# A two-layer perceiver kernel: the latents as chunk 0 of the second cross attention's loop, high and low parts of the first one rearranged, and a weight split placed later

## The chip, the cores and the metric

The kernel runs on one core of a Trainium2 chip. The metric is the device time of one execution in microseconds. Median before: 2354.21 us of 3 runs (2351.45 to 2356.31). The engines are called as the profile calls them, with their roles: PE is TensorE (matmuls), PEld its weight loads, DVE is VectorE, ACT is ScalarE, POOL is GpSimd, SP is SyncE, which only issues DMAs here.

## The reference

Four batches of 128 latents of width 512 (`x`) attend to a context of 4 x 2048 rows (`ctx_1024`). Six sublayers follow each other, each added to `x`; the three that the change touches are shown.

```python
# 1: cross attention with "stablemax", 16 heads of 32
def stablemax(x):
    s = jnp.where(x >= 0, x + 1.0, 1.0 / (1.0 - x))
    return s / jnp.sum(s, axis=-1, keepdims=True)
x = x + L0_xattn(layernorm(x), ctx)          # softmax replaced by stablemax
x = x + L0_attn(layernorm(x))                # causal linear attention
# 3: feed-forward with fake quantisation by the maximum of the whole tensor
def act_fake_quant(x, clip_factor):
    scale = jax.nn.sigmoid(clip_factor) * jnp.max(jnp.abs(x)) / 127.0
    return jnp.clip(round(x / scale), -128.0, 127.0) * scale
h = act_fake_quant(silu(gate(xq)) * up(xq), clip_down)
# 4: perceiver attention, 16 heads of 64
xn, ln = layernorm(x_ctx, g, b), layernorm(latents, g, b)
q = ln @ Wq
kv = jnp.concatenate((xn, ln), axis=1) @ Wkv  # context and latents are keys
sim = where(mask_full, q @ k.T * scale, -max) # the latents' part is unmasked
out = layernorm(softmax(sim) @ v @ Wout, g, b)
x = x + L1_attn(layernorm(x)); x = x + L1_ffn(layernorm(x))
```

## The kernel before, in words

Every sublayer is one or more `Block`s: each engine has its own instruction list in a block, and all engines meet at its end. Inside a block, engines wait for each other by semaphores only, and each engine keeps the order in which its list is written. Matmuls with fp32 accuracy are done as three fp16 ones: a value is scaled and rounded to a high part (`_hi`), what is left is the low part (`_lo`), and hi x hi, hi x lo and lo x hi are added in PSUM.

**First cross attention** (`context_attention_0`). 8192 context rows are taken in 16 chunks of 512. A chunk has 8 units (`UNITS`), each half of the heads for 128 keys, 1024 columns wide. Per unit u of chunk c: PE makes scores (L611) into one of two pairs of banks; ACT and DVE form stablemax as max(s+1, exp(-ln(1+relu(-s)))): Relu (L475), Ln (L478), Exp (L481) on ACT and the maximum with the scores on DVE (`larger`, L530). In units 2 and 6 (`MIN_ON_DVE`) DVE takes the minimum instead of ACT's Relu (L524), and ACT goes on with Ln (L471). POOL rounds the result to `p_hi` (L419); the low part `p_lo` is made by DVE (L537), in units 3 and 7 (`LOW_ON_POOL`) by POOL (L424). Three units later (`LAG`) PE multiplies by the values (L626). In the same stream PE projects keys and values of chunk c+1, one of 8 products per unit (L593, L597); ACT and DVE split each product (L452, L459; L507, L513). Context rows of chunk c+2 are split too, high part on POOL (L412, behind `p_hi` of units 1 to 4), low part on DVE (L500, in slots 4 to 7). DVE's list in slot u of a chunk is: minimum of u (if 2 or 6), `larger` of u-1, split of product u-1, low part of u-2, sums of the chunk before (slot 2), context low part (slots 4 to 7).

**Feed-forward of layer 0** (`quantised_ffn_0`, L972 to L1106). POOL's list: memset, first `partition_all_reduce` (the maximum over partitions), then for both next weights (`wk`, `wv` of the second cross attention) scale, round to high, subtract to low (L980, L983, L986), then the second `partition_all_reduce`. DVE waits for the second one, then quantises h in 22 scalar operations (L1058, L1061); ACT and PE follow.

**Second cross attention** (`context_attention_1`). After queries are made, a block of its own handles the latents as keys: 16 projections (8 of keys, 8 of values), then per batch plain scores for a running maximum (L1389), the maximum (L1463), a spread of it by DMA into a diagonal (L1326, L1318), scores less the maximum (L1292, L1300), exponential (L1441), `p_hi` on POOL (L1365), `p_lo` on DVE (L1493), outputs (L1310), copy to `acc` (L1485). A second block runs over 16 context chunks c. Ahead of its loop stand normalisation of chunks 0 and 1 (moments and a Newton step on DVE, L1674 to L1698, the scaling on POOL, L1553), their turn by PE (L1872), and the projections of chunk 0 with its plain scores (L1882). In iteration c, 16 units of chunk c (scores, Exp L1649, POOL L1584, DVE L1764, outputs) stand beside the 16 projections of chunk c+1 (`mm_keys` L1244, `mm_values` L1254, split by L1611, L1618, L1710, L1717), its plain scores, and the turn of chunk c+2. Products, plain scores and turns share a ring of 4 PSUM banks in a fixed order (`RING_ORDER`).

Of the kernel before, what the change touches and what calls it, by code (L numbers as in the profile page):

```python
# [5 lines left out]
P = 128  # L6
# [219 lines left out]
def context_attention_0(nc, g, d):  # L226
# [6 lines left out]
    MIN_ON_DVE = (2, 6)  # L233
    LOW_ON_POOL = (3, 7)
    with ExitStack() as ctx:
# [101 lines left out]
        with ExitStack() as sub:  # L337
# [15 lines left out]
            min_done, p_done, p_hi_done = s.sem("min_done"), s.sem("p_done"), s.sem("p_hi_done")  # L353
            low_v, low_p = s.sem("low_v"), s.sem("low_p")
            outputs, acc_done = s.sem("outputs"), s.sem("acc_done")

            ON_ACT = [u for u in range(UNITS) if u not in MIN_ON_DVE]
            LOW_ON_DVE = [u for u in range(UNITS) if u not in LOW_ON_POOL]

            def place(c, u, units):  # L360

                return len(units) * c + len([x for x in units if x <= u])

            def low_wait(eng, c, u):

                if u in LOW_ON_POOL:
                    eng.wait_ge(low_p, place(c, u, LOW_ON_POOL))
                else:
                    eng.wait_ge(low_v, place(c, u, LOW_ON_DVE))

# [9 lines left out]
            with nc.Block() as block:  # L380
# [25 lines left out]
                def _(pool):  # L406
# [15 lines left out]
                    def p_low(c, u):  # L422
                        pool.wait_ge(p_hi_done, UNITS * c + u + 1)
                        nc.gpsimd.tensor_tensor(p_lo[:, u % 4, :], r[:, u % 4, :], p_hi[:, u % 4, :], ALU.subtract)\  # L424
                            .then_inc(low_p, 1)

# [11 lines left out]
                    for c in range(NCH):  # L438
                        for u in range(UNITS):
                            p_high(c, u)  # L440
                            if u in LOW_ON_POOL:
                                p_low(c, u)
                            if c + 2 < NCH and 1 <= u < KT + 1:
                                context_hi(c + 2, u - 1)

                @block.scalar
                def _(act):
# [17 lines left out]
                    def below_zero(c, u):  # L465

                        if before(c, u, 4):
                            low_wait(act, *before(c, u, 4))
                        if u in MIN_ON_DVE:
                            act.wait_ge(min_done, place(c, u, MIN_ON_DVE))  # L470
                            nc.scalar.activation(r[:, u % 4, :], r[:, u % 4, :], ACT.Ln, scale=-1.0, bias=1.0)\  # L471
                                .then_inc(ln_done, 1)
                        else:
                            act.wait_ge(scores, UNITS * c + u + 1)
                            nc.scalar.activation(r[:, u % 4, :], bank_pair(u), ACT.Relu, scale=-1.0, bias=1.0)\  # L475
                                .then_inc(neg_done, 1)
                            act.wait_ge(neg_done, place(c, u, ON_ACT))
                            nc.scalar.activation(r[:, u % 4, :], r[:, u % 4, :], ACT.Ln, bias=1.0)\  # L478
                                .then_inc(ln_done, 1)
# [16 lines left out]
                def _(dve):  # L496
# [21 lines left out]
                    def below_zero(c, u):  # L518

                        if u in MIN_ON_DVE:  # L520
                            dve.wait_ge(scores, UNITS * c + u + 1)
                            if before(c, u, 4):
                                low_wait(dve, *before(c, u, 4))
                            nc.vector.tensor_scalar(r[:, u % 4, :], bank_pair(u), -1.0, 0.0, ALU.add, ALU.min)\  # L524
                                .then_inc(min_done, 1)

# [6 lines left out]
                    def p_low(c, u):  # L533
                        if u in LOW_ON_POOL:
# [3 lines left out]
                            .then_inc(low_v, 1)  # L538
# [14 lines left out]
                    for c in range(NCH):  # L553
                        for u in range(UNITS):
                            below_zero(c, u)
# [1930 lines left out]
```

## Time and profile before

| what | us |
|---|---|
| median of the runs shown | 2354.21 |
| the profiled execution, and its span | 2355.0, 2353.2 |
| loop of the first cross attention, from its first score | 90.85 to 633.4 |
| feed-forward block of layer 0 | 824.4 to 896.3 |
| block of the latents as keys | 950.3 to 1053.2 |
| context block up to its loop | 1053.5 to 1118.4 |
| its loop, 16 iterations | 1118.4 to 2037.3 |

Busy over the whole span: PE 85%, DVE 69%, ACT 41%, POOL 32%. How to read the rows: times are microseconds from the span's start. In a timeline a row is start, length, engine, line of the kernel, operation, output<-inputs, shapes, how many were merged, and in brackets how long the engine sat idle before and what released it. A row of busy time by stretch has the stretch and its length, then busy time and instructions of PE, PEld, DVE, ACT and POOL, the granted PE clock as a share of full speed (1.00 is 2.4 GHz, 0.50 is 1.2 GHz), the DMA engines' share and GB/s. L12 is line 12 of the kernel before.

### The profile page before, as it was taken

How to read it: one execution, taken by the hardware profiler on the slowest of the kernel's cores; microseconds unless marked ns; L12 is line 12 of the kernel's file. 1: busy time of each engine (PE TensorE's matmuls, PEld its weight loads, DVE VectorE, ACT ScalarE, POOL GpSimd, SP SyncE). 2: the span in 40 equal slices, each digit the busy share in tenths (PEclk: the TensorE clock that was granted, in tenths of full speed). 3: DMA queues.
4: the chain of work that ended last, by engine and by line, in shares of the span. 5: the costliest groups of instructions: out<-in, count | busy, mean ns of one | idle time of the engine just before them, and what ended most of it. 6: DMA issues, size and time to landing. Idle time of an engine off the chain costs nothing. (4 is left out here: it accounts for less than half of the span.)

```text
span 2353.2 us, 44141 instructions
## 1 busy us (share of the span) xinstructions
PE 1994.2 (85%) x17800; PEld 1095.5 (47%) x17800; DVE 1629.5 (69%) x2826; ACT 962.8 (41%) x1373; POOL 743.5 (32%) x736
## 2 busy tenths in 40 slices
PE   3788988898589346848999999999999999667896
PEld 1355555555445223334555555555555555434542
DVE  3489888988754764255777777777777776535676
ACT  2477787877610322212333333333333333201332
POOL 2355555564410350012333333333333332212010
PEclk8899999999689567968999999999999999988898
DMA  4223323331220401000000000000000000110300
GB/s 136 64 72 91 91 57 80 91 76 43 55 108 24 170 1 36 20 2 22 26 16 20 20 21 21 21 21 21 21 21 21 20 21 1 46 68 0 148 1 18
DMA packets 39194, 106.16 MB, mean 45 GB/s; under 512 B 18384, under 2 KB 20688, under 8 KB 32848
## 3 DMA queue, kind: packets, MB, share of 16 engines
q1 hardware_dynamic: 38992, 103.35, 14.2%
q8 instruction: 141, 2.31, 0.4%
q14 instruction: 61, 0.50, 0.1%
HBM read 75.42 MB, written 1.05 MB: 32 GB/s over the span
## 5 line engine op out<-in xcount | busy, mean ns | idle before, releaser
L1584 POOL TENSOR_SCALAR a1c_p_hi<-a1c_pf 128x512 f16<-128x512 f32 x256 | 191.1, 747 | 622.5 <-ACT a1c_pf L1649 621.1
L419 POOL TENSOR_SCALAR a0c_p_hi<-a0c_r 128x1024 f16<-128x1024 f32 x128 | 153.1, 1196 | 254.7 <-DVE a0c_r L530 188.1
L1611 ACT ACTIVATE a1c_k_hi<-PS 128x512 f16<-128x512 f32 x128 | 76.5, 598 | 305.7 <-PE PS L1244 305.7
L1649 ACT ACTIVATE a1c_pf<-PS,a_maskc 128x512 f32<-128x512 f32 x256 | 175.2, 686 | 48.8 <-PE PS L1300 38.5
L1764 DVE TENSOR_TENSOR a1c_p_lo<-a1c_pf,a1c_p_hi 128x512 f16<-128x512 f32 x256 | 185.8, 727 | 5.2 <-POOL a1c_p_hi L1584 5.2
L1732 DVE CUSTOM_DVE_ANT_0 a1c_junk<-PS,a1c_maskr 128x512 bf16<-128x512 f32 x256 | 175.9, 687 | 19.2 <-DVE a1c_ctop L1732 1.0
L1618 ACT ACTIVATE a1c_v_hi<-PS 128x512 f16<-128x512 f32 x128 | 76.9, 601 | 244.5 <-PE PS L1254 195.2
L1710 DVE SCALAR_TENSOR_TENSOR a1c_k_lo<-PS,a1c_k_hi 128x512 f16<-128x512 f32 x128 | 88.3, 690 | 99.9 <-ACT a1c_k_hi L1611 99.9
L530 DVE TENSOR_TENSOR a0c_r<-PS,a0c_r 128x1024 f32<-128x1024 f32 x128 | 155.1, 1211 | 2.0 <-ACT a0c_r L481 2.0
L537 DVE TENSOR_TENSOR a0c_p_lo<-a0c_r,a0c_p_hi 128x1024 f16<-128x1024 f32 x96 | 151.5, 1578 | 0.0
L1244 PE MATMUL PS<-a_x_hi,w_wk_hi 128*128 128x512 f16 x544 | 141.2, 382 | 9.2 <-PEq L1203 4.5
L1717 DVE SCALAR_TENSOR_TENSOR a1c_v_lo<-PS,a1c_v_hi 128x512 f16<-128x512 f32 x128 | 88.5, 692 | 86.2 <-ACT a1c_v_hi L1618 84.8
L1310 PE MATMUL PS<-a1c_v_hi,a1c_p_hi 128*128 128x65 f16 x1088 | 129.7, 196 | 19.8 <-DVE a_acc L1485 13.4
L1244 PE MATMUL PS<-a_x_lo,w_wk_hi 128*128 128x512 f16 x544 | 141.4, 383 | 0.0
L1244 PE MATMUL PS<-a_x_hi,w_wk_lo 128*128 128x512 f16 x544 | 140.5, 381 | 0.0
L1254 PE MATMUL PS<-w_wv_lo,a_x_hi 128*128 128x512 f16 x544 | 139.6, 379 | 0.0
L1254 PE MATMUL PS<-w_wv_hi,a_x_lo 128*128 128x512 f16 x544 | 139.6, 379 | 0.0
L1254 PE MATMUL PS<-w_wv_hi,a_x_hi 128*128 128x512 f16 x544 | 139.3, 378 | 0.0
L481 ACT ACTIVATE a0c_r<-a0c_r 128x1024 f32<-128x1024 f32 x128 | 135.5, 1058 | 4.1
L1310 PEld LDWEIGHTS PS<-a1c_v_hi,a1c_p_hi 128*128 128x128 f16 x1088 | 101.0, 98 | 64.6 <-issue 27.6
L1310 PE MATMUL PS<-a1c_v_hi,a1c_p_lo 128*128 128x65 f16 x1088 | 128.8, 196 | 0.0
L1310 PE MATMUL PS<-a1c_v_lo,a1c_p_hi 128*128 128x65 f16 x1088 | 127.7, 195 | 0.0
(367 smaller groups left out, 4969.1 us busy)
## 6 DMA issues: line engine op xcount, KB each, us to landing
a_cf<-in_ctxT SPq DMA_DIRECT2D x16, 1024.0 KB, 5.2
a0c_ks<-a0c_k_hi SPq DMA_DIRECT2D x128, 128.0 KB, 2.3
a1c_cf<-in_ctx SPq DMA_DIRECT2D x16, 1024.0 KB, 4.9
a0c_ks<-a0c_k_lo SPq DMA_DIRECT2D x64, 128.0 KB, 2.4
f_w<-in_w SPq DMA_DIRECT2D x4, 1024.0 KB, 8.8
f_w<-in_w SPq DMA_DIRECT2D x1, 4096.0 KB, 19.9
s1q_w<-in_L1a_wT SPq DMA_DIRECT2D x3, 1024.0 KB, 7.5
w_gate_raw<-in_w_gate SPq DMA_DIRECT2D x1, 2816.0 KB, 9.5
```

The source lines that it names most:

```text
L419: nc.gpsimd.tensor_scalar(p_hi[:, u % 4, :], r[:, u % 4, :], 1.0, 0.0, ALU.mult, ALU.add)\
L481: nc.scalar.activation(r[:, u % 4, :], r[:, u % 4, :], ACT.Exp, scale=-1.0)\
L530: nc.vector.tensor_tensor(r[:, u % 4, :], bank_pair(u), r[:, u % 4, :], ALU.max)\
L537: nc.vector.tensor_tensor(p_lo[:, u % 4, :], r[:, u % 4, :], p_hi[:, u % 4, :], ALU.subtract)\
L1244: mm = nc.tensor.matmul(out, wk[i][:, k, f * P:(f + 1) * P], (x_hi, x_lo)[j][e][:, k, :], start=(step == 0), stop=(step == 11))
L1254: mm = nc.tensor.matmul(out, (x_hi, x_lo)[j][e][:, k, t * P:(t + 1) * P], wv[i][:, k, group * BANK:(group + 1) * BANK], start=(step == 0), ...
L1310: mm = nc.tensor.matmul(out(h, i), p[:, n % 4, i * P:(i + 1) * P], v[e][:, t, h, :], start=(first(h) and step == 0), stop=(last(h) and ste ...
L1584: nc.gpsimd.tensor_scalar(p_hi[:, v % 4, :], pf[:, v % 2, :], 1.0, 0.0, ALU.mult, ALU.add)\
L1649: nc.scalar.activation(pf[:, v % 2, :], g.PS[:, S0 + v % 2, :], ACT.Exp, bias=maskc[:, at:at + 1]).then_inc(exp_done, 1)
L1717: nc.vector.scalar_tensor_tensor(out=v_lo[e][at], in0=g.PS[:, ring_bank("values", c, n), :].rearrange("p (h n) -> p h n", h=8), scalar=UNS ...
L1732: nc.vector.tensor_tensor_reduce(junk[:], g.PS[:, ring_bank("plain", c, h), :], maskr[c % 2][:], 1.0, LOWEST, ALU.add, ALU.max, ctop[:, h: ...
L1764: nc.vector.tensor_tensor(p_lo[:, v % 4, :], pf[:, v % 2, :], p_hi[:, v % 4, :], ALU.subtract)\
```

## The change

Three edits. In the first cross attention every unit now has the Relu on ACT and the low part on DVE; `MIN_ON_DVE`, `LOW_ON_POOL` and their semaphores go.

```diff
-    MIN_ON_DVE = (2, 6)
-    LOW_ON_POOL = (3, 7)
...
                         for u in range(UNITS):
                             p_high(c, u)
-                            if u in LOW_ON_POOL:
-                                p_low(c, u)
                             if c + 2 < NCH and 1 <= u < KT + 1:
                                 context_hi(c + 2, u - 1)
...
-                        if u in MIN_ON_DVE:
-                            act.wait_ge(min_done, place(c, u, MIN_ON_DVE))
-                            nc.scalar.activation(r[:, u % 4, :], r[:, u % 4, :], ACT.Ln, scale=-1.0, bias=1.0)\
-                                .then_inc(ln_done, 1)
-                        else:
...
+                        act.wait_ge(scores, UNITS * c + u + 1)
+                        nc.scalar.activation(r[:, u % 4, :], bank_pair(u), ACT.Relu, scale=-1.0, bias=1.0)\
+                            .then_inc(neg_done, 1)
+                        act.wait_ge(neg_done, UNITS * c + u + 1)
+                        nc.scalar.activation(r[:, u % 4, :], r[:, u % 4, :], ACT.Ln, bias=1.0).then_inc(ln_done, 1)
...
                     def p_low(c, u):
-                        if u in LOW_ON_POOL:
-                            return
                         dve.wait_ge(p_hi_done, UNITS * c + u + 1)
```

In the feed-forward the split of the second weight stands behind the second reduction instead of before it.

```diff
                 for i in range(2):
                     pool.wait_ge(top_done, i + 1)
                     nc.gpsimd.partition_all_reduce(tops[:, i:i + 1], top[:, i:i + 1], P, reduced_max)\
                         .then_inc(all_done, 1)
-                    if i == 0:
-                        for n, (hi, lo) in enumerate(g.next_weights):
...
+                    next_weights(i)
```

In the second cross attention the latents' block goes. The loop runs over j = 0 to 16 (`NJ`): j = 0 is the latents, j >= 1 is context chunk j-1. The latents are projected ahead of the loop, with the turn of context chunk 0 in slots 11 to 14, and the normalisation of one context chunk instead of two. In iteration 0, each unit's outputs are a sum of their own that DVE copies to `acc` (`first_sums`, 16 copies of 260 columns, where 12 of up to 455 stood); its tops have their own tiles, one diagonal per batch, 8 spread DMAs of 4 times the size, and no mask. PE waits for the memsets of the ones before its first projection.

```diff
+    NJ = NCH + 1
...
+                    pe.wait_ge(ones_set, 4)
                     for v in range(UNITS):
                         if v % 2 == 0 and v >= 2:
                             plain_scores(0, v // 2 - 1)
                         project(0, v)
...
+                    for j in range(NJ):
                         for v in range(UNITS):
                             if v % 2 == 0:
-                                score(c, v)
+                                score(j, v)
...
-                            if c + 1 < NCH:
-                                project(c + 1, v)
+                            if j + 1 < NJ:
+                                project(j + 1, v)
...
+                    def first_sums(v):
+
+                        t, gp, side = tile_of(v), group_of(v), side_of(v)
+                        dve.wait_ge(outputs, v + 1)
+                        nc.vector.tensor_copy(acc[:, batch_at(0, t), 8 * gp + side:8 * gp + 8:2, :],
+                                              g.PS[:, O0 + side, 0:4 * W].rearrange("p (h n) -> p h n", h=4))\
+                            .then_inc(acc_done, 1)
...
+                        if j == 0:
+                            for b in range(B):
+                                build_diag(diag0[b], topx0[:, :, b, :], fs).then_inc(diag_done, 1)
+                            return
...
+                            if j == 0 and v >= 4:
+                                first_sums(v - 4)
+                            if j == 1 and v < 4:
+                                first_sums(UNITS - 4 + v)
...
+                        if j == 0:
+                            first, last = True, True
+                            if v >= 2:
+                                pe.wait_ge(acc_done, v - 1)
```

## Rows read from the trace of the kernel before

**Rows 1.** Busy time by stretch: first loop, latents' attention, second loop

```profile
296.00:331.00 35.00, 31.27 (x379) 18.82 (x377) 32.05 (x32) 27.70 (x32) 19.18 (x14) 1.00 0.28 77
...
995.00:1053.00 58.00, 26.18 (x464) 20.85 (x464) 32.29 (x56) 9.12 (x16) 9.71 (x16) 0.65 0.02 2
...
1236.00:1296.00 60.00, 60.00 (x629) 32.52 (x628) 44.88 (x102) 22.79 (x39) 19.33 (x26) 1.00 0.08 25
```

**Rows 2.** Timeline of PE, first cross attention, one chunk

```profile
299.98 1.04 PE L593 MATMUL PS<-a0c_c_hi,a_wk_hi 128*128 128x512 f16 x4 [2.10 <-DVE a0c_c_lo L500]
...
323.12 0.62 PE L611 MATMUL PS<-a_qs,a0c_ks 98*128 98x128 f16 x8 [1.56 <-DVE a0c_r L530]
...
333.78 1.04 PE L593 MATMUL PS<-a0c_c_hi,a_wk_hi 128*128 128x512 f16 x4 [2.10 <-DVE a0c_c_lo L500]
```

**Rows 3.** Timeline of DVE, first cross attention, the same chunk

```profile
301.58 1.21 DVE L537 TENSOR_TENSOR a0c_p_lo<-a0c_r,a0c_p_hi 128x1024 f16<-128x1024 f32 x1
...
307.48 1.22 DVE L524 TENSOR_SCALAR a0c_r<-PS 128x1024 f32<-128x1024 f32 x1 [2.95 <-PE PS L611]
308.62 1.21 DVE L530 TENSOR_TENSOR a0c_r<-PS,a0c_r 128x1024 f32<-128x1024 f32 x1
...
314.37 1.68 DVE L537 TENSOR_TENSOR a0c_p_lo<-a0c_r,a0c_p_hi 128x1024 f16<-128x1024 f32 x1
...
319.30 2.62 DVE L500 SCALAR_TENSOR_TENSOR a0c_c_lo<-a_cf,a0c_c_hi 128x512 f16<-128x512 f32 x1
...
323.58 1.15 DVE L500 SCALAR_TENSOR_TENSOR a0c_c_lo<-a_cf,a0c_c_hi 128x512 f16<-128x512 f32 x1
```

**Rows 4.** Timeline of ACT, first cross attention, unit 1 of that chunk

```profile
303.90 1.03 ACT L475 ACTIVATE a0c_r<-PS 128x1024 f32<-128x1024 f32 x1 [0.51 <-PE PS L611]
...
306.04 1.06 ACT L481 ACTIVATE a0c_r<-a0c_r 128x1024 f32<-128x1024 f32 x1
```

**Rows 5.** Timeline of POOL, first cross attention, unit 3 of that chunk

```profile
318.40 2.98 POOL L424 TENSOR_TENSOR a0c_p_lo<-a0c_r,a0c_p_hi 128x1024 f16<-128x1024 f32 x1
```

**Rows 6.** Timeline of POOL, feed-forward layer of layer 0

```profile
830.93 0.38 POOL L975 PARTITION_ALL_REDUCE f_tops<-f_top  x1 [6.31 <-DVE f_top L1027]
838.15 3.60 POOL L980 TENSOR_SCALAR f_raw<-f_raw 128x4096 f32<-128x4096 f32 x1 [6.84 <-issue]
...
845.56 8.02 POOL L986 TENSOR_TENSOR w_wk_lo<-f_raw,w_wk_hi 128x4096 f16<-128x4096 f32 x1
...
874.69 0.38 POOL L975 PARTITION_ALL_REDUCE f_tops<-f_top  x1 [5.82 <-issue]
```

**Rows 7.** Timeline of DVE, feed-forward layer of layer 0

```profile
838.64 7.11 DVE L1042 TENSOR_SCALAR f_diag<-g_ident,f_sd 128x128 f32<-128x128 f32 x4
...
862.39 0.17 DVE L1055 TENSOR_REDUCE f_top<-f_hmax 128x1 f32<-128x11 f32 x1
...
884.59 0.43 DVE L1061 TENSOR_SCALAR f_hT<-f_hT 128x512 f32<-128x512 f32 x1
```

**Rows 8.** Timeline of PE, second cross attention: projections and loop starts

```profile
950.31 1.82 PE L1244 MATMUL PS<-a_x_hi,w_wk_hi 128*128 128x512 f16 x4 [4.53 <-PEq L1203]
...
1068.18 1.89 PE L1244 MATMUL PS<-a_x_hi,w_wk_hi 128*128 128x512 f16 x4 [3.36 <-DVE a_x_lo L1703]
...
1118.43 0.39 PE L1292 MATMUL PS<-a1c_diag,a_negones 64*128 64x512 bf16 x2
...
1236.42 0.39 PE L1292 MATMUL PS<-a1c_diag,a_negones 64*128 64x512 bf16 x2
...
1295.97 0.39 PE L1292 MATMUL PS<-a1c_diag,a_negones 64*128 64x512 bf16 x2
```

**Rows 9.** Timeline of POOL, then of DVE, second cross attention's two blocks

```profile
950.81 0.70 POOL L1360 MEMSET a1c_v_lo<- 128x64 f16 x1
...
1057.79 0.16 DVE L1698 SCALAR_TENSOR_TENSOR a1c_nmr<-a1c_mv,a1c_rstd 128x4 f32<-128x4 f32 x1
```

**Rows 10.** The page's part 6: DMA issues of the second context

```profile
a1c_cf<-in_ctx SPq DMA_DIRECT2D x16, 1024.0 KB, 4.9
```

More of the change, by code:

```diff
@@ L1510, in context_attention_1 @@
             outputs, scaled, acc_done = s.sem("outputs"), s.sem("scaled"), s.sem("acc_done")
-            topx_in = s.sem("topx_in")
-            def whole(chunk):
-                for c in range(NCH):
-                    chunk(c, c % 2)
+            topx_in, side_done, ones_set = s.sem("topx_in"), s.sem("side_done"), s.sem("ones_set")
             with nc.Block() as block:
@@ L1592, in _ @@
-                    whole(chunk)
+                            if j + 1 < NCH and v == 9:
+                                normalise(j + 1)
+                            if j + 1 < NCH and v == 11:
+                                mask_row(j + 1)
+                            if j + 1 < NCH and v > TURN:
+                                context_hi(j + 1, v - TURN - 1)
                 @block.scalar
@@ L1596, in context_f32 @@
                     def context_f32(c, k):
-                        act.wait_ge(turned, 4 * c + k + 1)
-                        if at_least(c, 1) or k >= 2:
-                            act.wait_ge(x_lo_done, 4 * c + k - 1)
-                        bank = S0 + k if first(c) else ring_bank("turn", c, k)
-                        nc.scalar.activation(xf[:, k % 2, :], g.PS[:, bank, :], ACT.Identity,
+                        act.wait_ge(turned, KT * c + k + 1)
+                        if c >= 1 or k >= 2:
+                            act.wait_ge(x_lo_done, KT * c + k - 1)
@@ L1665, in _ @@
-                    whole(chunk)
+                    for v in range(UNITS):
+                        evacuate(0, v)
+                        if TURN <= v < TURN + KT:
+                            context_f32(0, v - TURN)
+                    for j in range(NJ):
+                        for v in range(UNITS):
+                            if j + 1 < NJ and v >= 1:
+                                evacuate(j + 1, v - 1)
+                            if j + 1 < NCH and v > TURN:
+                                context_f32(j + 1, v - TURN - 1)
+                            probability(j, v)
+                            if j + 1 < NCH and v == 8:
+                                inverse_root(j + 1)
+                            if j >= 1 and v == 5:
+                                shrink(j)
+                        if j + 1 < NJ:
+                            evacuate(j + 1, UNITS - 1)
@@ new lines, in _ @@
+                            if j + 1 < NCH and v in (1, 3, 5, 7):
+                                moments(j + 1, (1, 3, 5, 7).index(v))
+                            if j + 1 < NCH and v == 8:
+                                newton_step(j + 1)
+                            if j + 1 < NCH and v > TURN:
+                                context_lo(j + 1, v - TURN - 1)
+                        if j + 1 < NJ:
+                            split_lo(j + 1, UNITS - 1)
+                    p_low(NCH, UNITS - 1)
@@ L1918, in _ @@
                     LAG = 3
-                    for k in range(KT):
-                        turn(0, k)
+                    pe.wait_ge(ones_set, 4)
                     for v in range(UNITS):
```

737 lines of the change are left out of this document (280 added, 457 removed).

## The prediction

> **What bounds the kernel now.** I read the granted clock and the busy time by stretch first, then the timeline of each engine in the three stretches that the diff touches, and in each asked which wait ends last. The kernel is a chain of stages behind barriers, so what a stage gains or loses reaches the end whole. Busy shares by stretch tell three stories [rows 1]. In the first cross attention's loop TensorE, VectorE and ScalarE are all close to full (31.27, 32.05 and 27.70 of 35 us). In the second one's loop TensorE alone is full (60.00 of 60 us). Between the two lies the latents' own attention, where TensorE works 26.18 of 58 us at a mean granted clock of 0.65: nothing is full there, and the time is handed from engine to engine.
>
> **First cross attention: the loop's period.** One chunk takes 33.80 us: TensorE's first key projection starts at 299.98 and at 333.78, each time released by VectorE's low part of the context, L500, after an idle 2.10 us; once more, at 323.12, it waits 1.56 us for L530 [rows 2]. So TensorE has 33.80 - 2.10 - 1.56 = 30.1 us of work in a chunk. VectorE idles once, 2.95 us before the minimum L524 of unit 2 (at 307.48), and then runs without a gap until it releases TensorE [rows 3]. That closes the loop: projection, score, VectorE's string of work, low part of the context, projection. What counts is the length of this string.
>
> What the change does to it, by the starts of successive rows:
> - The minimum of unit 2 goes. Today `larger` of unit 1 starts at 308.62, behind it [rows 3]. Its input, the Exp of unit 1, starts at 306.04 and takes 1.06 us [rows 4], so it could start at 307.16, with the 0.06 us that such a hand-over takes. Gain 1.46 us.
> - The minimum of unit 6 goes, it lies inside the string: 1.13 us (starts of 307.48 and 308.62 [rows 3]).
> - The low part of unit 3 comes over from GpSimd to VectorE. The row says 1.68 us with GpSimd beside it and 1.21 us where it is not held [rows 3]; the next instruction starts some 0.07 earlier, so 1.61 or 1.13. GpSimd's own high part starts just ahead of each, so I take 1.61. The low part of unit 7 comes over as well, in slot 1 of the next chunk, but there VectorE has 2.95 us of idle time and it hides: at its full 1.61 us still 0.6 us are left before `larger` of unit 1.
> - GpSimd's low part, 2.98 us at 318.40 [rows 5], is what the context's low part at 319.30 sits behind: 2.62 us, where its sister at 323.58 takes 1.15 [rows 3]. After the change GpSimd runs a short context high part there, and I price it as the sister: 1.48 us less. The ends are 0 (something else holds it as long) and 2.5 (nothing of it is left).
>
> Sum: -1.46 - 1.13 + 1.61 - 1.48 = -2.46 us, period 31.34 us. Is another engine late next? TensorE's 30.1 is under it. ScalarE has 27.70 x 33.8/35 = 26.75 us in a chunk [rows 1] and gets two Relus of 1.03 us [rows 4]: 28.8, under it, though no longer loose. VectorE is then idle for well under 1 us in a chunk, so it is the bound, with TensorE 1.2 us behind. The string with the context's low part stands in 14 chunks (the last two load none): 14 x 2.46 = **34.4 us less**. The last chunk is ScalarE's: two more Relus (+2.1 at most) against two waits for the minimum and a last low part on the faster engine (1.21 for 2.98 us [rows 3, 5]): 0. Ends: 14 x (1.46 + 1.13 - 1.61) = 13.7 us less if the context's part is not relieved, 14 x 3.66 = 51 less if TensorE's own work becomes the bound.
>
> **The weight split.** Today GpSimd reduces the first maximum (830.93), starts the splits 6.84 us after it, at 838.15, takes 15.4 us for one weight (two of these fill 838.15 to 868.9), and starts the second reduction 5.82 us later, at 874.69 [rows 6]. VectorE had the maximum at 862.39 + 0.17 = 862.56 [rows 7], so 12 us pass in which VectorE, TensorE and ScalarE wait. With one weight moved, GpSimd is free at 853.6. Its changeover of 5.8 us then lies before the maximum is there, as for the first reduction, which starts 0.35 us after its input [rows 6, 7]. The second reduction would end at 862.56 + 0.35 + 0.38 = 863.3 instead of 875.1: **11.8 us earlier**.
>
> But the moved split follows at once and meets VectorE's quantisation, 22 scalar operations of 0.43 us [rows 7]. The trace shows such a meeting: four smaller ones (L1042) beside these very splits took 7.11 us, from 838.64 to the end of GpSimd's second instruction near 845.5 [rows 6, 7]. So about two get through for each of GpSimd's instructions, and the next is held until that instruction ends. After the reduction GpSimd needs its 6.84 us again, so it starts at 870.1; 15 of the 22 are done by then. The other 7 go: two at each of the two gaps, and three behind the 8.02 us subtraction [rows 6]. The split ends at 870.1 + 15.4 = 885.5, the last of the 22 at 886.8; before it was 884.59 + 0.43 = 885.0 [rows 7]. Net **+1.8 us**: the early reduction is given back. Ends: -11.8 if nothing is held, +4 if only one gets through at a gap and the additions to x are held too.
>
> Here the notes have two rules to weigh. The Trainium skill, Advanced Engine Details and Errata, section VectorE Performance Modes, says that GPSIMD instructions and VectorE's two-port ones "will interfere/block eachother"; an SBUF to SBUF scalar operation in fp32 is such a one, and the 7.11 us at L1042 agree. The Trainium skill, GPSIMD Engine Reference, section Instruction dispatch, puts a load of about 6 us before the first call of a freshly loaded kernel; the gap of 5.82 agrees, but by it alone nothing would be paid after the reduction, where the row has 6.84. By that section alone the split would run from 863.3 to 878.7, 16 operations would be left, and the term would be +0.6 instead of +1.8.
>
> **Second cross attention.** Now the latents have a block of their own: projections from 950.31, attention to 1053, then the first context chunk's normalisation and turn, its projections from 1068.18, and the loop from 1118.43; a full iteration takes 1295.97 - 1236.42 = 59.55 us of TensorE's time [rows 8]. After the change the latents are projected with the first chunk's turn in the stream, and their 16 units run beside the projection of the first context chunk, as one more iteration of the same loop. The 16 units' own work does not change in kind; their idle time gets a projection to fill it.
> - Start to loop. The projections of chunk 0 with plain scores and turns took 1118.43 - 1068.18 = 50.25 us, both starts at the lower clock level (four matmuls in 1.8 to 1.9 us) [rows 8]. The latents' now have the same form. Before the first stands a new wait for four memsets, the last at 950.81 + 0.70 [rows 9], +1.2 us; behind it all of TensorE's stream is queued. VectorE and ScalarE have the first chunk's moments ahead of the first split: the load lands 4.9 us after its issue [rows 10], moments to Newton step took 4.4 us (1053.53 to 1057.95 [rows 9]), so the first split starts near 959.6, where the third projection waits for it: +0.7. The four diagonals at slot 11 in place of one, and a spread of four times as many small pieces: between 0 and 4 us, I take 1, since the ring holds four banks. Loop start 950.3 + 1.2 + 50.25 + 1.7 = 1003.5, which is 114.9 earlier.
> - One more iteration: +59.55.
> - In it VectorE, 44.88 of 60 us busy [rows 1], gets 16 copies of the sums for the scaling and four additions (about 5 us more) and four more diagonals (2.7 us): 88% busy, still under TensorE, so 0; for bursts at slot 3 I put +1, with 0 to 8 as ends.
> - The other iterations are the same instructions under new numbers: 0.
>
> Sum -114.9 + 59.55 + 1 = **54.4 us less**, ends 60 and 43.
>
> **Total.** -34.4 + 1.8 - 54.4 = -87.0. The profiled execution took 2355.0 us (span 2353.2 and 1.8 around it), 0.8 over the median of the runs shown; so **2268.0 us**, with 2259 to 2280 as this case's own range.
>
> **Rivals.**
> 1. *VectorE isn't relieved in the first loop.* The context's low part is held as long by GpSimd's high parts, which now run there. For: 2.62 us has been seen only beside GpSimd. Against: the sister's 1.15 beside a high part. First loop -13.7: 2288.7. Chance 0.15.
> 2. *VectorE's low parts run free* (1.13) and TensorE is the bound: -51, 2251. Against: the high part that holds them starts just ahead of each. Chance 0.10.
> 3. *The early reduction is kept*, since VectorE gets through between GpSimd's instructions: -11.8 in place of +1.8: 2254.4. Chance 0.12; the row of L1042 speaks against it.
> 4. *The copies don't replace what they should*: the latents' units wait for VectorE's copies bank by bank in the new iteration. 16 waits of 0.7 us: 2279, inside the forecast's range. Chance 0.03, counted with it.
> 5. *Slower than before.* TensorE's clock drops in the second loop. An iteration of 59.55 us of matmuls at 1.2 GHz takes up to 59.55 more; a share of 87/59.55 = 1.5 iterations in 17 decides. If three ran so: 2268 + 179 = 2447. Against: the level stood at 1.00 where TensorE had no gap [rows 1], and it fell only where it idled. Chance 0.02.
>
> **How the numbers follow.** Forecast with rival 4: 0.61; the others 0.15, 0.10, 0.12, 0.02. The range 2252 to 2291 takes in the forecast's and rivals 1 and 3; rival 2 and 5 lie outside (0.12). What a measurement here can tell from no change is about 0.2%, 4.7 us. All but rival 5 lie far below: faster 0.97, same 0.01, slower 0.02.
>
> **What would show it.** First loop: starts of L593 after L500 31.3 us apart, the wait for L530 gone, the longest L500 near 1.1 us. Feed-forward: the reduction ending 0.7 us after its maximum, and then VectorE's scalar operations held to 3.6 and 8 us (the length of GpSimd's instructions). Second: loop start some 53 us after the block's, 17 iterations, all at 59.5 or a little over. I am wrong if the last low part in a chunk isn't what releases the projection, or if an iteration grows by even 1 us, which would cost 17.

## The result and the profile after

Median 2265.39 us of 4 runs (2261.59 to 2266.41) against 2354.03 (2351.45 to 2356.31): ratio 0.9615, 95% interval 0.9603 to 0.9627. Forecast: 2268.0. The profiled execution took 2266.4 us with a span of 2264.6, 88.6 us less than before's; the forecast's sum was 87.0 less.

The span by stage, with marks that both kernels have (first score, the reciprocal behind each loop, the memset of ones, the memset of `negones`, the memsets of the second cross attention):

| stage | before | after | difference | forecast |
|---|---|---|---|---|
| up to the first score | 90.85 | 91.41 | +0.6 | 0 |
| first cross attention's loop | 543.58 | 507.05 | -36.5 | -34.4 |
| linear attention, layer norm | 189.99 | 190.41 | +0.4 | 0 |
| feed-forward block | 72.94 | 76.09 | +3.2 | +1.8 |
| queries | 52.91 | 53.17 | +0.3 | 0 |
| second cross attention: start to loop | 168.16 | 53.75 | -114.4 | -114.9 |
| its loop | 919.13 | 979.08 | +60.0 | +60.6 |
| the rest | 315.64 | 313.64 | -2.0 | 0 |

Of the 2.0 us at the end 1.7 are clock, in unchanged code: near the end of the last feed-forward the same group of matmuls takes 5.40 us in before (at 2334.99) and 3.70 in after (at 2248.06).

**First loop.** Timeline of PE in the trace of after, one chunk apart (start, length, engine, line, operation, output<-inputs, how many merged, and in brackets the idle time and its releaser):

```profile
285.01 0.82 PE L552 MATMUL PS<-a0c_c_hi,a_wk_hi 128*128 128x512 f16 x3 [1.89 <-DVE a0c_c_lo L471]
...
316.22 0.60 PE L552 MATMUL PS<-a0c_c_hi,a_wk_hi 128*128 128x512 f16 x2 [1.90 <-DVE a0c_c_lo L471]
```

The answer to [rows 2]: period 31.21 us instead of 33.80, the wait for the banks of the scores is gone, that for the context's low part is left. VectorE in the same chunk, the answer to [rows 3]:

```profile
292.16 1.23 DVE L492 TENSOR_TENSOR a0c_r<-PS,a0c_r 128x1024 f32<-128x1024 f32 x1 [1.01 <-ACT a0c_r L452]
...
301.25 1.68 DVE L497 TENSOR_TENSOR a0c_p_lo<-a0c_r,a0c_p_hi 128x1024 f16<-128x1024 f32 x1
302.85 1.09 DVE L471 SCALAR_TENSOR_TENSOR a0c_c_lo<-a_cf,a0c_c_hi 128x512 f16<-128x512 f32 x1
...
307.20 1.09 DVE L471 SCALAR_TENSOR_TENSOR a0c_c_lo<-a_cf,a0c_c_hi 128x512 f16<-128x512 f32 x1
```

One idle time in a chunk, 1.01 us before `larger` of unit 1, then no gap until the low part that releases TensorE. The low part of unit 3 takes 1.68 us (301.25), and the context's low part behind it 1.09 instead of 2.62. So VectorE's string still closes the loop.

**Feed-forward.** VectorE from the second maximum on, the answer to [rows 7], then GpSimd, the answer to [rows 6]:

```profile
827.11 0.17 DVE L1015 TENSOR_REDUCE f_top<-f_hmax 128x1 f32<-128x11 f32 x1
...
834.74 0.43 DVE L1021 TENSOR_SCALAR f_hT<-f_hT 128x512 f32<-128x512 f32 x1
835.09 3.91 DVE L1018 TENSOR_SCALAR f_hT<-f_hT,f_inv 128x512 f32<-128x512 f32 x1
839.03 3.70 DVE L1021 TENSOR_SCALAR f_hT<-f_hT 128x512 f32<-128x512 f32 x1
842.65 8.14 DVE L1018 TENSOR_SCALAR f_hT<-f_hT,f_inv 128x512 f32<-128x512 f32 x1
850.82 0.43 DVE L1021 TENSOR_SCALAR f_hT<-f_hT 128x512 f32<-128x512 f32 x1
...
851.68 0.43 DVE L1021 TENSOR_SCALAR f_hT<-f_hT 128x512 f32<-128x512 f32 x1
```

```profile
827.41 0.38 POOL L944 PARTITION_ALL_REDUCE f_tops<-f_top  x1 [9.15 <-DVE f_top L1015]
835.11 3.59 POOL L935 TENSOR_SCALAR f_raw<-f_raw 128x4096 f32<-128x4096 f32 x1 [7.32 <-issue]
838.79 3.66 POOL L938 TENSOR_SCALAR w_wv_hi<-f_raw 128x4096 f16<-128x4096 f32 x1
842.53 7.97 POOL L940 TENSOR_TENSOR w_wv_lo<-f_raw,w_wv_hi 128x4096 f16<-128x4096 f32 x1
```

The reduction comes 0.3 us behind its maximum, as forecast, and 16 of the 22 quantisation operations run free. Then each of three ends 0.3 us behind the GpSimd instruction beside it: 3.91, 3.70 and 8.14 us for work of 0.43 to 0.48. From the maximum to the next block's first memset it is 37.85 us now and was 34.97.

**Second cross attention.** PE: first projection, third projection, and the starts of iterations 0, 1 and 2 (the answer to [rows 8]):

```profile
919.42 1.03 PE L1214 MATMUL PS<-a_x_hi,w_wk_hi 128*128 128x512 f16 x2 [5.78 <-POOL a1c_v_lo L1342]
...
929.29 1.04 PE L1214 MATMUL PS<-a_x_hi,w_wk_hi 128*128 128x512 f16 x4 [0.71 <-DVE a1c_k_lo L1475]
...
971.88 0.39 PE L1711 MATMUL PS<-a1c_diag,a_negones 64*128 64x512 bf16 x2
...
1030.33 0.39 PE L1711 MATMUL PS<-a1c_diag,a_negones 64*128 64x512 bf16 x2
...
1089.88 0.39 PE L1711 MATMUL PS<-a1c_diag,a_negones 64*128 64x512 bf16 x2
```

Busy time in iteration 0 (columns as in [rows 1]), then in the first iteration of before's loop:

```profile
971.88:1030.33 58.45, 58.45 (x595) 31.55 (x595) 46.31 (x108) 21.24 (x38) 18.30 (x25) 1.00 0.08 23
```

```profile
1118.43:1176.88 58.45, 58.45 (x591) 31.37 (x590) 43.13 (x98) 22.89 (x39) 19.45 (x26) 1.00 0.07 23
```

TensorE has no gap in either. An iteration that stands first is 1.1 us shorter than the next, in both kernels: its first three units have no outputs of an iteration before them. VectorE is 79% busy in iteration 0.

### The profile page after: what moved, and what is told of

Same layout as the page of the kernel before. It is cut to its first block and busy times, and to the rows that moved or that the text cites. A ratio compares the mean times of both kernels' runs of the same rounds, so it can differ in the third digit from the quotient of the medians.

```text
span 2264.6 us, 44140 instructions
## 1 busy us (share of the span) xinstructions
PE 1973.3 (87%) x17797; PEld 1085.4 (48%) x17800; DVE 1633.7 (72%) x2842; ACT 994.9 (44%) x1404; POOL 679.4 (30%) x704
## 5 line engine op out<-in xcount | busy, mean ns | idle before, releaser
L1352 POOL TENSOR_SCALAR a1c_p_hi<-a1c_pf 128x512 f16<-128x512 f32 x272 | 201.6, 742 | 666.0 <-ACT a1c_pf L1408 623.5
L1377 ACT ACTIVATE a1c_k_hi<-PS 128x512 f16<-128x512 f32 x136 | 81.2, 597 | 326.8 <-PE PS L1214 326.8
L497 DVE TENSOR_TENSOR a0c_p_lo<-a0c_r,a0c_p_hi 128x1024 f16<-128x1024 f32 x128 | 202.4, 1581 | 0.9 <-POOL a0c_p_hi L403 0.9
L1557 DVE TENSOR_TENSOR a1c_p_lo<-a1c_pf,a1c_p_hi 128x512 f16<-128x512 f32 x272 | 198.2, 730 | 6.0 <-POOL a1c_p_hi L1352 6.0
L1384 ACT ACTIVATE a1c_v_hi<-PS 128x512 f16<-128x512 f32 x136 | 81.6, 600 | 258.8 <-PE PS L1224 206.0
L492 DVE TENSOR_TENSOR a0c_r<-PS,a0c_r 128x1024 f32<-128x1024 f32 x128 | 155.3, 1213 | 24.9 <-ACT a0c_r L452 24.7
L1475 DVE SCALAR_TENSOR_TENSOR a1c_k_lo<-PS,a1c_k_hi 128x512 f16<-128x512 f32 x136 | 93.8, 689 | 106.3 <-ACT a1c_k_hi L1377 106.3
L1482 DVE SCALAR_TENSOR_TENSOR a1c_v_lo<-PS,a1c_v_hi 128x512 f16<-128x512 f32 x136 | 94.0, 691 | 86.7 <-ACT a1c_v_hi L1384 85.3
L450 ACT ACTIVATE a0c_r<-a0c_r 128x1024 f32<-128x1024 f32 x128 | 135.4, 1058 | 4.1
L452 ACT ACTIVATE a0c_r<-a0c_r 128x1024 f32<-128x1024 f32 x128 | 135.3, 1057 | 4.1
L447 ACT ACTIVATE a0c_r<-PS 128x1024 f32<-128x1024 f32 x128 | 130.9, 1023 | 7.3 <-PE PS L570 7.2
```

What stands on the lines that cost most here:

```text
L452: nc.scalar.activation(r[:, u % 4, :], r[:, u % 4, :], ACT.Exp, scale=-1.0)\
L492: nc.vector.tensor_tensor(r[:, u % 4, :], bank_pair(u), r[:, u % 4, :], ALU.max)\
L1352: nc.gpsimd.tensor_scalar(p_hi[:, v % 4, :], pf[:, v % 2, :], 1.0, 0.0, ALU.mult, ALU.add)\
L1557: nc.vector.tensor_tensor(p_lo[:, v % 4, :], pf[:, v % 2, :], p_hi[:, v % 4, :], ALU.subtract)\
```

## Experiments

All are the kernel after with one thing changed, unless said otherwise, and are timed against the kernel before on the same chip; ratios are to before. The theory is the prediction's: in the first loop the minimum is the gain, in the feed-forward the hold eats the earlier reduction, and in the second cross attention it is idle time of TensorE that went.

**split_undone**: both splits ahead of the second reduction again.

```diff
-                    next_weights(i)
+                    if i == 0:
+                        for n in range(2):
+                            next_weights(n)
```

> The kernel after, with the feed-forward edit undone: both weight splits stand ahead of the second reduction again. My theory: the moved split holds VectorE's quantisation, one operation for each of GpSimd's three instructions (3.91, 3.70 and 8.14 us in the trace of after), and this gives the early reduction back and 3 us more. So this kernel is 3.1 us faster than after, 2262 us; from the memset of ones to the next block's first memset 72.9 us instead of 76.1. Rival: the earlier reduction is worth its 11.8 us somewhere behind the block (an earlier start of a load), and undoing it costs time: 2265 to 2277 us.

Measured 2262.45 us, ratio 0.9613 (0.9598 to 0.9627); its profile has 73.24 us for the block and 35.06 from the maximum to its end, against 76.09 and 37.85. The whole times of the two kernels overlap, and the block's length doesn't decide it either: seven other kernels below, whose feed-forward is after's, take 73.4 to 75.9 us for it. The stretch behind the maximum does: 36.9 to 37.9 us in the eight profiles with the moved split, 35.0 and 35.1 in before and here. So the moved split costs 1.9 to 2.9 us, and the pair compared first stands at the upper end. No stage behind the block is more than 0.2 us shorter in after, which ends the rival.

**split_waits**: the second split behind the quantisation.

```diff
+                    if i == 1:
+                        pool.wait_ge(hc_done, FT0)
                     next_weights(i)
```

> The kernel after, but GpSimd waits for VectorE's last quantisation operation before it begins the second weight's split. Theory: holding is the whole cost. The 22 operations take 9.4 us without a hold and end some 10 us after the maximum; GpSimd's gap of 7.3 us lies beside them, its split of 15.3 us then runs beside TensorE's down projection and ends the block: maximum + 10.5 + 15.3 + 1.2, so the block is 65.3 us long instead of 76.1, 10.8 less, 2254.6 us. If the additions to x, which read SBUF twice, are held as well, the last ones come behind the 8 us subtraction: 3 us of it are lost, 2257.5. Rival: the three long VectorE operations have another cause than GpSimd (a semaphore, the port of the maximum): they stay at 3.7 to 8.1 us, and GpSimd ends later still: 2265 to 2280 us.

Measured 2256.87 us, 0.9589 (0.9571 to 0.9607); 67.32 us for the block, 29.65 from the maximum to its end. The quantisation runs free, so nothing but GpSimd had held it. The branch of the expectation in which the additions are held came true. VectorE, then GpSimd, in the trace of split_waits:

```profile
848.65 0.69 DVE L1030 TENSOR_TENSOR f_y<-PS,f_sdb 128x512 f32<-128x512 f32 x1
849.37 7.59 DVE L1032 TENSOR_TENSOR g_x<-g_x,f_y 128x512 f32<-128x512 f32 x1
856.88 0.68 DVE L1030 TENSOR_TENSOR f_y<-PS,f_sdb 128x512 f32<-128x512 f32 x1
```

```profile
840.47 3.61 POOL L935 TENSOR_SCALAR f_raw<-f_raw 128x4096 f32<-128x4096 f32 x1 [10.05 <-DVE f_hT L1023]
844.16 3.92 POOL L938 TENSOR_SCALAR w_wv_hi<-f_raw 128x4096 f16<-128x4096 f32 x1
848.16 8.25 POOL L940 TENSOR_TENSOR w_wv_lo<-f_raw,w_wv_hi 128x4096 f16<-128x4096 f32 x1
```

The addition with both inputs in SBUF, 0.69 us when it is free, waits 7 us for the end of GpSimd's subtraction. The product before it, with one input in PSUM, takes its 0.69 beside the same subtraction. The Trainium skill, SBUF — State Buffer, section SBUF: two separate sides, says this: a port pair shared by the two engines, locked for a whole instruction, which VectorE wants in its two-port modes and with two SBUF inputs. The trace agrees in both respects.

**min_alone and low_alone**: the two halves of the first loop's edit, in before's version of `context_attention_0`; the rest is as after.

```diff
-    MIN_ON_DVE = (2, 6)
+    MIN_ON_DVE = ()
...
-    LOW_ON_POOL = (3, 7)
+    LOW_ON_POOL = ()
```

The first hunk alone is min_alone, the second alone is low_alone.

> The kernel after, but in the first cross attention only half of the edit: all Relus on ScalarE, while GpSimd keeps the low parts of units 3 and 7. By the steps of my prediction the minimum is the whole gain (1.46 + 1.13 = 2.59 us in a chunk), and the low part on VectorE (+1.61) and the relief of the context's low part (-1.48 to -1.59) cancel: period 31.2 us and 2265 us, within 3 of after. The longest context low part is 2.6 us again. Rival: what helped is that GpSimd no longer holds VectorE: then most of the 36 us are gone, 2290 to 2301 us.

> The other half alone: VectorE keeps the minimum of units 2 and 6, all low parts are on VectorE. By my steps this is worth +1.61 - 1.59 = 0.0 us in a chunk: period 33.8 us and 2301 us, with VectorE's low part of unit 7 partly outside its idle time, up to 5 more. Rival (relief of VectorE from GpSimd is the gain): 2265 to 2280 us, period 31 to 32.

Measured: min_alone 2255.64 us, 0.9584 (0.9568 to 0.96); low_alone 2304.91, 0.9783 (0.9757 to 0.9808). The periods are 31.18 and 33.82 us. So in the period the minimum is the whole gain, and moving the low parts is worth nothing, as the steps had it. PE, then VectorE, then GpSimd in the trace of min_alone:

```profile
316.69 1.04 PE L593 MATMUL PS<-a0c_c_hi,a_wk_hi 128*128 128x512 f16 x4 [1.48 <-DVE a0c_c_lo L500]
```

```profile
292.66 1.23 DVE L530 TENSOR_TENSOR a0c_r<-PS,a0c_r 128x1024 f32<-128x1024 f32 x1 [2.61 <-ACT a0c_r L481]
...
303.35 2.61 DVE L500 SCALAR_TENSOR_TENSOR a0c_c_lo<-a_cf,a0c_c_hi 128x512 f16<-128x512 f32 x1
```

```profile
302.44 2.97 POOL L424 TENSOR_TENSOR a0c_p_lo<-a0c_r,a0c_p_hi 128x1024 f16<-128x1024 f32 x1
```

The context's low part is held for 2.61 us again, and the period is none the longer. But min_alone is 9.8 us faster than after, where I had written "within 3": over the whole kernel, moving the low parts to VectorE was a loss. By stages of the two profiles: 3.2 us in the loop, 5.5 in the linear attention behind it, 2.7 in the feed-forward block, all with the same period or the same code. The granted clock differs. Busy time by stretch of after, then of min_alone, each the loop from 100 to 560 us and then the linear attention:

```profile
100.00:560.00 460.00, 432.95 (x5104) 260.34 (x5102) 436.41 (x434) 420.66 (x469) 216.12 (x172) 0.99 0.31 82
...
598.46:788.87 190.41, 130.99 (x500) 73.11 (x500) 113.24 (x174) 31.09 (x53) 30.56 (x29) 0.79 0.27 101
```

```profile
100.00:560.00 460.00, 437.26 (x5148) 262.68 (x5147) 416.19 (x407) 425.49 (x472) 276.63 (x202) 1.00 0.32 83
596.45:781.38 184.93, 125.28 (x500) 71.47 (x500) 113.01 (x174) 31.08 (x52) 30.59 (x28) 0.81 0.27 104
```

After has three chunks of 32.8 us among its 14, with a mean clock of 0.83 in the 10 us from 252; min_alone has none. The seven profiles whose first loop is after's (TensorE idle 1.9 us in each chunk) show three to five such chunks each and 506.6 to 511.2 us for the loop; before and low_alone (idle 2.1 and another 1.5 us) show three and two. Min_alone (idle 1.5 once) and the four with less idle time have the full clock up to 545 us. That the idle time brings the dips is argued from these fourteen profiles, not shown: no run changed it alone. Why the linear attention, whose code is the same, is 5.5 us shorter stays open.

**context_low_earlier**: the context's low parts one slot earlier.

```diff
-                            if c + 2 < NCH and u >= 4:
-                                context_lo(c + 2, u - 4)
+                            if c + 2 < NCH and 3 <= u < KT + 3:
+                                context_lo(c + 2, u - 3)
```

> The kernel after, with VectorE's four context low parts of the first cross attention one slot earlier (slots 3 to 6 of a chunk instead of 4 to 7). Nothing is left out or added. If, as I hold, the last of them is what releases TensorE's first projection (1.89 us idle in each of 14 chunks), TensorE is now released by the split of product 6, which stands 2.3 us earlier in VectorE's list. TensorE's own work is 31.21 - 1.89 = 29.3 us in a chunk, VectorE's 31.21 - 1.01 = 30.2: period 30.2 to 30.4 us, 11 to 14 us less, 2252 us. Rival: VectorE's string from `larger` of unit 1 to the chunk's end is as long in any order and closes through the scores' banks: period 31.2, 2265. Second rival: GpSimd's high part isn't there yet in slot 3 and VectorE waits up to 1.5 us for it: 2265 to 2286.

Measured 2246.35 us, 0.9547 (0.9529 to 0.9565), 19 us under after; period 30.52. PE, and the busy time by stretch, in its trace:

```profile
304.57 0.62 PE L570 MATMUL PS<-a_qs,a0c_ks 98*128 98x128 f16 x8 [0.39 <-DVE a0c_r L492]
```

```profile
296.00:331.00 35.00, 34.55 (x426) 21.09 (x424) 35.00 (x35) 33.24 (x38) 17.79 (x15) 1.00 0.39 98
```

The wait of 1.9 us is gone, and VectorE is busy for 35.00 of 35 us. So it was VectorE's string, through this low part, that bounded after's loop. The period is 0.1 over the expected range, since a third context low part now lies beside a GpSimd instruction (1.09 instead of 0.68). The loop is 492.0 us long, 15.1 less: 14 x 0.69 = 9.7 are the period, and the rest is mostly that the long chunks are gone, which I had not forecast. The linear attention is shorter again, 184.3 us for 190.4.

**latents_undone**: before's `context_attention_1` in the kernel after.

> The kernel after, with the second cross attention of before: the latents have a block of their own again. Theory: this part alone is worth what the trace of after shows, 54.5 us (114.4 from the block's start to the loop's, less 59.9 for a longer loop): 2319.9 us, and the stages before the block don't change by more than their clock does, some 3 us. Rival: a part of the gain that I put down to it belongs to the stages around (their granted clock, loads that start earlier): 2300 to 2315 us.

Measured 2316.86 us, 0.9848 (0.9834 to 0.9863). Its second cross attention takes 1087.28 us, after's 1032.83: 54.45 us, all of it in the stage itself. The whole times differ by 51.5 only and the two profiled spans by 48.4: with unchanged code its linear attention is 6.4 us and its feed-forward block 2.2 us shorter than after's, and its first loop 3.7 longer. The linear attention takes 184.0 to 190.4 us in the fourteen profiles of this study, so a theory about 3 us is not to be tested on the whole time.

**ones_later and moments_later**: what stands ahead of the second loop. In ones_later:

```diff
                         if j == 0:
                             first, last = True, True
+                            if v == 0:
+                                pe.wait_ge(ones_set, 4)
...
-                    pe.wait_ge(ones_set, 4)
                     for v in range(UNITS):
```

In moments_later this and:

```diff
-                    for t in range(NT):
-                        moments(0, t)
-                    newton_step(0)
                     for v in range(UNITS):
                         if v >= 1:
                             split_lo(0, v - 1)
...
+                        if v == 2:
+                            for t in range(NT):
+                                moments(0, t)
+                        if v == 4:
+                            newton_step(0)
```

with ScalarE's `inverse_root(0)` behind the third product's rounding.

> The kernel after, with TensorE's wait for the four memsets moved from the first projection of the second cross attention to its first output. Theory: the wait in front is on the path, and with it goes 1.2 us: first projection at 0.1 us behind the block's start instead of 1.3, loop start 1.2 earlier, 2264.2 us. Rival: the third projection waits for VectorE's first split behind the moments (0.7 us today), which comes no earlier: the 1.2 us are only moved there, 2265.4.

> The kernel after, with TensorE's wait for the memsets moved to its first output as in ones_later, and with the first context chunk's moments and Newton step (VectorE, and ScalarE's two small operations) moved behind the split of the latents' second product. Theory after ones_later: in after, the third projection (11.16 us behind the block's start) waits for VectorE's first split, and this one stands in line behind the context load and the moments; the memsets are hidden under that. So with both moved the third projection starts some 8.1 us behind the block's start, as in the kernel before, and the loop 50.7 to 51.2 us behind it instead of 53.75: 3 us less, 2262.4 us. Rival: TensorE runs at its lower level when it is released early, as in ones_later (54.85), and loses what it gains: 53 to 55, 2265.

Measured: ones_later 2265.64 us, 0.9623 (0.9606 to 0.964), 54.85 us from the block's start to the loop, 1.1 more than after's 53.75; moments_later 2264.55, 0.9612 (0.9594 to 0.963), 50.86 us. PE of ones_later, whose block starts at 911.20:

```profile
911.24 1.83 PE L1214 MATMUL PS<-a_x_hi,w_wk_hi 128*128 128x512 f16 x4 [4.53 <-PEq L1173]
...
920.94 0.40 PE L1679 MATMUL PS<-a1c_k_hi,a_q_hi 64*128 64x128 f16 x8 [2.68 <-ACT a1c_k_hi L1377]
922.05 1.46 PE L1214 MATMUL PS<-a_x_hi,w_wk_hi 128*128 128x512 f16 x3 [0.71 <-DVE a1c_k_lo L1475]
```

The wait only moved: 1.2 us less at the first projection, 2.68 instead of 0.51 us before the plain scores, and a third projection only 0.3 us earlier. Behind this longer gap the clock fell to its lower level again (three matmuls in 1.46 us; the row at 285.01 in after has 0.82 for three). The 1.1 us more are not the edit's: copies_twice, whose code up to the loop is after's, takes 55.42 us, with 2.01 us before the plain scores and a mean clock of 0.66 in the 5 us behind them, and the other eight profiles with this code 53.6 to 53.9. With the moments out of the way the third projection starts 8.1 us behind the block's start, at 927.40 in moments_later, and 2.9 us are gained in the stage. In the whole time they can't be seen.

**copies_twice**: each of the 16 copies of the latents' sums is done a second time into a spare tile.

```diff
                         dve.wait_ge(outputs, v + 1)
...
+                        for i in range(2):
+                            if i < 1:
+                                if v >= 1:
+                                    dve.wait_ge(copied, v)
+                                nc.vector.tensor_copy(spare[:],
+                                                      g.PS[:, O0 + side, 0:4 * W].rearrange("p (h n) -> p h n", h=4))\
+                                    .then_inc(copied, 1)
+                            else:
+                                cp = nc.vector.tensor_copy(acc[:, batch_at(0, t), 8 * gp + side:8 * gp + 8:2, :],
+                                                           g.PS[:, O0 + side, 0:4 * W].rearrange("p (h n) -> p h n", h=4))
+                        cp.then_inc(acc_done, 1)
```

> The kernel after, with a second copy of each of the latents' 16 sums into a spare tile, ahead of the real one: 16 more VectorE instructions of 0.33 us or a little more in iteration 0. Theory: VectorE works 45 of 56 us there and TensorE waits for none of it, so 5.3 us more are hidden: iteration 0 stays 58.4 to 58.8 us, 2265. Rival (the copies stand on the path through the accumulating banks, with two units of lag): each costs its 0.33 us: iteration 0 grows to 63.7, 2270.7.

Measured 2261.78 us, 0.9614 (0.9598 to 0.963). Iteration 0:

```profile
965.84:1024.30 58.46, 58.46 (x597) 31.55 (x596) 50.95 (x120) 21.22 (x38) 18.25 (x25) 1.00 0.08 24
```

4.6 us more on VectorE (12 of the 16 fall into this stretch) and 0.01 on the iteration: the copies are hidden, and the +1 us that I had put down for bursts isn't there.

**combined_a, combined_b, combined_c**: the first loop as in min_alone with `context_lo` one slot earlier, and the feed-forward as in split_waits; in b `LOW_ON_POOL = (7,)` instead of (3, 7); c is b with the two edits of moments_later.

> What the runs so far speak for, together, on the kernel after: first cross attention with all Relus on ScalarE, the low parts of units 3 and 7 on GpSimd, and the context low parts one slot earlier; feed-forward with the second split behind the quantisation. VectorE's work in a chunk is then 31.18 - 2.61 = 28.6 us, TensorE's 29.7 to 30.1: TensorE becomes the bound, period 29.7 to 30.2 us, 14 x 1.0 to 1.5 under the 31.2 of after, and 2 to 5 us more if TensorE's clock doesn't dip because it never idles. With 8 us from the feed-forward: 2265.4 - 18 - 8 = 2239, down to 2230. Rival: GpSimd's low part of unit 3 (2.97 us) now holds the second context low part and makes VectorE late for the banks of the scores: period 30.5 as in context_low_earlier, 2238 to 2242.

> As combined_a, but the low part of unit 3 is on VectorE and only that of unit 7 on GpSimd, where VectorE has idle time. By my rows a wash for VectorE (1.6 us more of its own work, 1.5 less of being held): period 29.7 to 30.2 us, 2230 to 2239, within 3 us of combined_a. Rival (one low part more on VectorE fills it): 30.5 us, 2238 to 2242.

> combined_b with the moments and the memset wait of the second cross attention placed as in moments_later. Theory: each stage keeps what it showed alone: first loop with a period of 30.15 us, from the second maximum to the feed-forward's end 29.6 us, and 50.9 us instead of 53.7 from the block's start to the second loop. That is 2.9 us less than combined_b: 2230.6 us, 34.8 under after. Rival: the stages in between, whose granted clock moved their length by up to 6 us from run to run, swallow it: 2233 to 2237.

Measured: a 2239.79 us, 0.9512 (0.9499 to 0.9525), period 30.54; b 2233.47, 0.9484 (0.9471 to 0.9497), period 30.15; c 2230.78, 0.948 (0.9467 to 0.9493), with 488.1, 66.35 and 50.10 us in the three stages. In a, TensorE still waits 1.09 us in a chunk for `larger`: GpSimd's low part of unit 3 holds VectorE, and the rival was right. In b, 6.3 us under a where I had expected at most 3, it waits 0.27; PE, and the busy time by stretch:

```profile
302.46 0.62 PE L611 MATMUL PS<-a_qs,a0c_ks 98*128 98x128 f16 x8 [0.27 <-DVE a0c_r L530]
```

```profile
296.00:331.00 35.00, 34.67 (x404) 20.77 (x402) 33.85 (x34) 33.52 (x38) 20.18 (x16) 1.00 0.40 101
```

TensorE is the bound there, but for this wait. The low part of unit 3, worth nothing in the period of after, is worth 0.4 us once the context low parts stand one slot earlier. c beats before and after both, by 123 and 35 us; its lead over b is within the intervals.

## Why the prediction held, step by step

- **What bounds the first loop**: right. The string VectorE, low part of the context, projection was still last in after, and taking that low part off it moved the bound (context_low_earlier).
- **Terms of the period**: forecast -2.46, measured -2.59. The start of `larger` of unit 1: from the projection to it 8.64 us before, 7.15 after, so -1.49 for -1.46. From it to the next projection 25.16 and 24.06, so -1.10 for -1.13 + 1.61 - 1.48 = -1.00: two context low parts became shorter (2.62 and 1.15 to 1.09 each), not one. Min_alone and low_alone confirm that the minimum carries all and the low parts cancel in the period. The 0.6 us left before `larger` of unit 1, and with it "idle for well under 1 us", was a slip: in the trace of before VectorE is free at 304.53, and 1.61 us later it is 306.14, 1.0 before 307.16. Measured is 1.01.
- **The last chunk at 0** and the clock's dips: the loop lost 36.5 us where 14 x 2.59 is 36.3. Both kernels have three long chunks (4.2 us in before, 4.9 in after), so the dips cancelled. That is luck: I had not thought of them, and in the seven profiles with this loop they cost 4.4 to 7.4 us, in five others nothing.
- **The weight split**: sign and mechanism right, size off. From the maximum to VectorE's last quantisation operation it was 22.6 us in before and is 25.0 in after (24.9 to 25.0 in all eight profiles with this order), +2.4 for +1.8. From there to the block's end it is 0.5 more in after, where the eight range from 12.0 to 12.9 us with unchanged code. The step that failed is "about two get through for each of GpSimd's instructions". I had it from the four operations of L1042, merged into one row of 7.11 us. Taken one by one they are 3.19, 0.27, 3.62 and 0.27 us: a held one, and then one short one that still fits in the gap. L1042's are 128 wide; the quantisation's are 512 wide, and of those only the held one got through. In after the wrong count cost nothing, since the gap behind the reduction was 7.32 us instead of 6.84 and let a 16th through free, so that three were left behind the subtraction, as in the sum. The 0.6 us that the sum lacks are this gap (+0.5, with a reduction 0.2 earlier than priced) and the 0.3 by which a held operation ends behind GpSimd's.
- **Start of the second loop**: 53.75 us behind the block's start, forecast 53.2, but by terms that partly cancelled. The +1.2 for the memsets is hardly on the path (ones_later: 0.3 of it): the third projection waits for the context load and the moments in any case. That chain I had priced too low: the load landed 6.1 us after its issue where the page's median says 4.9 [rows 10], and the third projection started at 11.16 us instead of 10.0. A maximum of two chains was written as a sum. The diagonals and spreads cost 0.45 us, forecast 1.
- **The added iteration**: +59.95 for +60.55; bursts cost nothing (copies_twice).
- **The total**: 2.6 us from the median, and this close partly by luck. I had put the linear attention at 0. It took 190.0 us in before and 190.4 in after, but 184.0 to 188.5 in eleven of the other twelve profiles.
- **Rivals**: 1, 2 and 5 are excluded by the periods and by the clock of 1.00 in the second loop, 3 by the held rows, 4 by an iteration 0 without a wait of TensorE.

## What to carry to other kernels

Ask of each engine's string between two releases which item ends it, and move that item ahead before giving work to another engine: one slot for four instructions took 15 us off this loop, 9.7 of them by the period, where the edit itself took 36. Don't set long GpSimd instructions beside VectorE operations that read and write SBUF alone; let them wait until those are done. Where two waits end near each other, price the later, not both.

## What the runs showed of the hardware

- A VectorE operation with SBUF operands alone that meets a GpSimd instruction ends behind that one by nearly its own free length: 0.3 us for a quantisation operation of 0.43 (which so took 3.70 to 8.14), 0.5 for a context low part of 0.68 (2.62) and for an addition of 0.69 (7.59), 1.1 for a low part of 1.21 (1.68). The product with an input in PSUM took its 0.69 beside the same instruction. Of quantisation operations, 512 wide, one got through for each GpSimd instruction in eight profiles; of the 128 wide ones of L1042, two in all fourteen.
- GpSimd's gap behind a `partition_all_reduce` (6.7 to 7.3 us) isn't added to a wait that stands behind it: in split_waits the split began 0.1 us after VectorE's last quantisation operation. The Trainium skill, GPSIMD Engine Reference, section Instruction dispatch, has about 6 us ahead of the first call of freshly loaded code. The traces have 5.82 and 5.91 us ahead of the reduction where its input was there, and the gap on the way back to ordinary instructions is longer. That both are loads of code is not shown by any run.
- The granted clock in stages where TensorE idles is not the same for the same code: 0.78 to 0.81 on average in the linear attention, 184.0 to 190.4 us, in different kernels. What sets it stays open.
